# Attention, MLP and rotation dealt from one list of lines; normalisation with z on ScalarE, and fp32 transposes split into high and low halves as they leave PSUM

## What is computed

```python
# each of the three layers; shift, scale and gate: six rows per sequence from silu(cond) @ w_ada
h = layernorm(x) * (1 + scale1) + shift1
x = x + gate1 * (attention(h, 16 heads of 18) @ w_proj)
h = layernorm(x) * (1 + scale2) + shift2
# layer 0: 4 experts of 288 -> 1152 -> 288, weighted by the top 2 of 4 gates; layers 1 and 2: one MLP
x = x + gate2 * (gelu(h @ w1 + b1) @ w2 + b2)
# last: E = expm(skew matrix of silu(c) @ W.T + b), U from the QR decomposition of P, computed on the chip
out = x + (x @ U) @ ((E - 1) @ U.T)
```

## Time and profile before

| what | before |
|---|---|
| median of three runs | 1694.19 us (1693.63 to 1696.64) |
| the profiled execution's own time | 1697.5 us |
| its span, first to last instruction | 1695.8 us |
| mean granted TensorE clock | 0.917 |
| TensorE matmul busy | 1415.2 us, 83% of the span |
| DVE busy | 1051.0 us, 62% |
| ScalarE busy | 804.6 us, 47% |
| GpSimd busy | 346.3 us, 20% |
| HBM traffic | 61 GB/s over the span |

### The profile page before, as it was taken

How to read it: one execution, slowest core, us unless ns; L and a number is a source line. 1 busy time by engine, 2 the same in 40 slices (tenths; PEclk the granted TensorE clock), 3 DMA queues, 4 the chain that set the end, 5 groups by cost and what they waited for, 6 DMA issues and landing times. The chain is left out here.

```text
span 1695.8 us, 31116 instructions
## 1 busy us (share of the span) xinstructions
PE 1415.2 (83%) x12102; PEld 822.2 (48%) x12102; DVE 1051.0 (62%) x2500; ACT 804.6 (47%) x1519; POOL 346.3 (20%) x425
## 2 busy tenths in 40 slices
PE   3647897787899997999999999899886657897877
PEld 0324453443555553556566555565643424454445
DVE  4566654667687777766665464655656775667443
ACT  1443454365455656564625555545454442453542
POOL 0001031223323333223111222211220020121210
PEclk9768998888899998999999999999998878898988
DMA  4332233422111212123103123202020010100001
GB/s 129 87 129 69 63 97 104 152 97 70 59 41 72 80 55 71 48 87 108 17 27 99 52 87 108 57 33 68 8 67 18 19 60 6 33 7 19 19 21 43
DMA packets 79465, 105.35 MB, mean 62 GB/s; under 512 B 39237, under 2 KB 66390, under 8 KB 75990
## 3 DMA queue, kind: packets, MB, share of 16 engines
q1 hardware_dynamic: 77206, 100.99, 19.3%
q10 hardware_dynamic: 2112, 2.36, 0.4%
HBM read 86.57 MB, written 16.49 MB: 61 GB/s over the span
## 5 line engine op out<-in xcount | busy, mean ns | idle before, releaser
L1204 PE MATMUL P<-XT,W 128*128 128x512 f16 x1512 | 355.9, 387 | 0.4 <-ACT HQS L1949 0.4
L1350 PE MATMUL P<-W,H 128*128 128x288 f16 x864 | 255.9, 296 | 2.0 <-POOL H L2011 1.9
L1351 PE MATMUL P<-W,H 128*128 128x288 f16 x864 | 255.0, 295 | 0.0
L1352 PE MATMUL P<-W,H 128*128 128x288 f16 x864 | 254.8, 295 | 0.0
L2006 POOL TENSOR_TENSOR X<-X,TM 128x288 f32<-128x288 f32 x144 | 126.9, 884 | 602.2 <-DVE TM L1683 513.5
L1204 PEld LDWEIGHTS P<-XT,W 128*128 128x128 f16 x1512 | 142.9, 99 | 178.9 <-issue 27.6
L1941 ACT ACTIVATE G<-P 128x512 f32<-128x512 f32 x216 | 129.0, 597 | 120.5 <-PE P L1204 104.4
L1931 ACT ACTIVATE ARENA<-P 128x512 f32<-128x512 f32 x256 | 135.5, 602 | 86.9 <-PE P L1310 86.7
L1608 DVE TENSOR_REDUCE NM<-P 128x2 f16<-128x512 f32 x256 | 157.8, 685 | 15.1 <-PE P L1295 14.7
L2011 POOL TENSOR_TENSOR H<-G,H 128x512 f16<-128x512 f32 x100 | 120.2, 1205 | 194.4 <-ACT H L1942 189.5
L1204 PE MATMUL P<-WQ,XT 128*128 128x288 f16 x1008 | 145.7, 289 | 1.2 <-ACT XT L1863 0.5
(11 more groups left out here) (283 smaller groups left out, 2240.2 us busy)
## 6 DMA issues: line engine op xcount, KB each, us to landing
W<-scr_w SPq DMA_DIRECT2D x9, 1440.0 KB, 6.1
W<-scr_w SPq DMA_DIRECT2D x9, 1368.0 KB, 5.7
ADB<-scr_ada SPq DMA_DIRECT2D x24, 432.0 KB, 4.1
ADB<-scr_ada SPq DMA_DIRECT2D x24, 288.0 KB, 4.3
scr_w<-W SPq DMA_DIRECT2D x4, 1440.0 KB, 5.9
scr_w<-W SPq DMA_DIRECT2D x4, 1368.0 KB, 5.7
STG<-in_L_w SPq DMA_DIRECT2D x11, 432.0 KB
STG<-in_L_WT SPq DMA_DIRECT2D x11, 324.0 KB
```

The source lines that it names most:

```text
L1204: ins = e.matmul(o, l, r, start=k == 0, stop=k == len(pairs_) - 1)
L1350: e.matmul(o, hi, W2[:, 2 * m, :], start=False, stop=False)
L1351: e.matmul(o, hi, W2[:, 2 * m + 1, :], start=False, stop=False)
L1352: ins = e.matmul(o, lo, W2[:, 2 * m, :], start=False, stop=m == 8)
```

## The change

It has two parts.

The order. `attention`, `across` and `fence` go. One `deal` runs over seven lines and the MLP stream until nothing is left: all attentions in order of layer and batch (rank 0), what follows them (`settle` and `finish`, 0.5), the maxima (0.8), the preparations (1), the background (3) and two lines of the rotation (5). The stream's `up` has rank 2 and its `down` -1. A line may split into several (a tuple is yielded): q, k and v of both tiles run as six, the maxima as two. `slot` and `two` now also yield until the time at which the bank is reckoned free. `hold` and `release` let the exponentials of an attention (half of one in layers 0 and 2) and the GELUs of an `up` take turns. Buffers that one line holds for another are marked None until they are free. The arena shrinks by XB, and Z, MB and OUT of the rotation move to the two staging buffers STG, so that the rotation of a batch may begin when its chunk has left the last MLP.

The columns. `layernorm` makes z = x * r - mean * r on ScalarE, one pass per tile with scale and bias per token; GpSimd computes the bias in two more small instructions; the scale is one DVE pass over both tiles (576 elements), the shift one more on DVE or GpSimd, whichever the planner reckons sooner. `to_columns` transposes y in fp32, six transposes into two banks, and the split into high and low is made in reading PSUM: ScalarE writes the high half to XT, DVE subtracts it and writes the low half and the copy of the 32 last features. The rows of ones in XT are set once (`xt_ones`).

```diff
 def slot(ring):
-    while ring.held():
-        yield "wait"
+    return slots(ring, 1)
...
+def slots(ring, n):
+    asked = -1.0
+    while True:
+        free = sorted((f for f in ring.free if f is not None), key=ends)
+        if len(free) < n:
+            yield "wait"
+        elif ends(free[n - 1]) <= asked or not free[n - 1]:
+            return
+        else:
+            asked = ends(free[n - 1])
+            yield list(free[n - 1])
...
+        Z = [STG[i][0:D, 0:256] for i in range(2)]
+        MB = [STG[i][0:D, 256:256 + C] for i in range(2)]
+        OUT = [STG[i][:, 544:544 + 2 * C].rearrange("p (a c) -> p a c", c=C) for i in range(2)]
...
+        def hold(kind):
+            other = "gelu" if kind == "exp" else "exp"
+            turns["asks"].add(kind)
+            while turns["now"] or (turns["last"] == kind and (other in turns["asks"] or other == "gelu" and ms.half == 0 and ms.line())):
+                yield "wait"
+            turns["asks"].discard(kind)
+            turns["now"] = turns["last"] = kind
...
+        def to_columns(b, y, full, mixed=False):
+            yield from two(rP)
+            _, j, pf = rP.take()
+            _, j2, pf2 = rP.take()
+            m = do(pe, "xb_T", 0.7, y=y, js=(j, j2), full=full, free=[pf, pf2])
+            yield [m]
+            before = TR[2 * b] + TR[2 * b + 1]
+            hi = do(act, "x_hi", 1.0, b=b, mixed=mixed, js=(j, j2), src=m, free=before)
+            yield [hi]
+            lo = do(dve, "x_lo", 1.3, b=b, mixed=mixed, js=(j, j2), src=m, hi=hi, free=before)
...
-            p = do(pool, "ln_eps", 0.4, w=w, src=aggr, free=tok.get(("mv", w)))
+            p = do(pool, "ln_eps", 0.6, w=w, src=aggr, free=tok.get(("mv", w)))
             p = do(pool, "ln_pow", 0.8, w=w, src=p)
+            p = do(pool, "ln_mean", 0.4, raises="ln_pow", w=w, src=p)
+            z = do(act, "ln_z", 1.2, w=w, b=b, power=p, x=[XW[2 * b], XW[2 * b + 1]], free=free)
+            s = do(dve, "ln_scale", 0.76, w=w, sc=sc, src=z, rows=rows)
+            lane, cost = sooner([s], (pool, 1.5), (dve, 0.76))
+            r = do(lane, "ln_shift", cost, raises=f"ln_shift_{lane.name}", w=w, sh=sh, src=s)
...
-        def deal(need, others=(), stream=False):
-            while not all(x.over for x in need):
+        def deal(lines):
+            while True:
+                todo = [y for x in (*lines, *ms.line()) for y in x.tips()]
...
+        every = [(L, b) for L in range(3) for b in range(B)]
+        preps = Line(chain(*(chain(*[wq_load(L)] * (L > 0), *(prep(L, b) for b in range(B))) for L in range(3))), 1)
+        tops = Line(chain(*(maxima_tokens(b) if L == 1 else maxima_rows(L, b) for L, b in every)), 0.8)
+        attends = Line(chain(*(attend_tokens(b) if L == 1 else attend(L, b) for L in range(3) for b in range(B))), 0)
+        deal([attends, ends_, tops, preps, bg, *(Line(rotated(k), 5) for k in range(2))])
...
             def xb_T(st):
+                for n in range(2):
+                    for k in range(2):
+                        c = 256 * k + 128 * n
+                        e.transpose(P[j][:, c:c + 128], y[:, n, 128 * k:128 * k + 128], IDF[:, :])
+                    ins = e.transpose(P[j2][0:32, 128 * n:128 * n + 128], y[:, n, 256:C], IDF[:, :])
...
+            def x_lo(st):
+                for k, part_ in main:
+                    e.tensor_tensor(like(st, XT[:, 3:5, :][:, k, sl]), part_, like(st, XT[:, 0:2, :][:, k, sl]), ALU.subtract)
+                e.tensor_tensor(like(st, low), tail, like(st, high), ALU.subtract)
+                e.tensor_copy(same, high).then_inc(st.sem)
...
+            def ln_z(st):
+                e.activation(YL[w][:, 0, :], X[:, 2 * b, :], ACT.Identity, scale=RSS[w][:, 1, 0:1], bias=RSS[w][:, 0, 0:1])
+                e.activation(YL[w][:, 1, :], X[:, 2 * b + 1, :], ACT.Identity, scale=RSS[w][:, 1, 1:2], bias=RSS[w][:, 0, 1:2]).then_inc(st.sem)
```

More of the change, by code:

```diff
@@ L96, in chain @@
         yield from p
+def slots(ring, n):
[9 more added lines that the diff above has]
+            yield list(free[n - 1])
 def slot(ring):
-    while ring.held():
-        yield "wait"
+    return slots(ring, 1)
 def two(ring):
-    while sum(f is not None for f in ring.free) < 2:
-        yield "wait"
+    return slots(ring, 2)
 def part(g, n):
@@ L247, in program @@
         V1 = over([2, C])
-        XB = [over([2, 640], F16) for _ in range(2)]
         YL = [over([2, C]) for _ in range(2)]
@@ new lines, in prep_tokens, with maxima_tokens, maxima @@
+            while qt_rd[u] is None:
+                yield "wait"
+            yield tuple(turned(g, *x) for g in range(2) for x in (("q", full_q, qb_rd, qt_rd[u]), ("k", full_k, kb_rd, kt_rd[u])))
+            tok["turned", 1, b] = made
+            qt_rd[u] = kt_rd[u] = v32_rd[u] = None
+            yield
+        def maxima_tokens(b):
+            while ("turned", 1, b) not in tok:
+                yield "wait"
+            u, made, mx = b % 2, tok["turned", 1, b], []
+            def maxima(first):
+                for c in range(first, 4, 2):
+                    yield from two(rP)
@@ new lines, in heads @@
+                while qt_rd[u] is None:
+                    yield "wait"
+                yield from slot(rP)
+                _, j, pf = rP.take()
+                m = do(pe, "qk_T", mm_cost(8, 128), name=name, n=n, j=j, src=[a, d], free=pf, ind=tok.get("ind"))
+                last[n] = [m]
+                yield [m]
+                v = copy("qt" if name == "q" else "kt", 1.03 + BIAS, 0.7, u=u, n=n, j=j, src=m, free=(qt_rd if name == "q" else kt_rd)[u])
+                rP.free[j] = [v]
+                made.append(v)
@@ L1083, in wait, with line @@
                     yield "wait"
-            def line(self, half=None):
-                if half is not None and half != self.half:
-                    return []
+            def line(self):
                 if self.now is not None and not self.now.over:
@@ L1090, in line @@
                 if self.able():
-                    self.now = Line(self.piece(), 9)
+                    self.now = Line(self.piece(), 2 if self.half == 0 else -1)
                     return [self.now]
@@ L1113, in step @@
                     return
+                if isinstance(v, tuple):
+                    self.kids = [Line(g, self.rank) for g in v]
+                    for x in self.kids:
+                        x.when = self.when
+                    return
                 self.when = self.before if v == "free" else ends(v) if isinstance(v, list) else newest[0]
                 self.before = newest[0]
-        def deal(need, others=(), stream=False):
-            while not all(x.over for x in need):
-                lines = [x for x in (*need, *others, *(ms.line() if (stream() if callable(stream) else stream) else ())) if not x.over]
-                now = [x for x in lines if x.when <= pe.clock + SLACK]
-                best = min(now, key=lambda x: x.rank) if now else min(lines, key=lambda x: x.when)
-                best.step()
@@ L1124, in attention @@
-        def attention(L, before, first, after):
-            deal([first, *before], [bg], stream=L > 0)
-            for b in range(B):
-                fin = Line(finish(L, b - 1) if b else iter(()), 2 if L == 2 else 0, tok["o", b - 1] if b else ())
-                nxt = Line(prep(L, b + 1), 1) if b + 1 < B else after
-                at = attend(L, b)
-                for n in (16, 99):
-                    if L == 0:
-                        deal(ms.line(1), [fin, nxt, bg])
-                    deal(ms.line(0), [fin, nxt, bg])
-                    deal([Line(part(at, n), 0)], [fin, nxt, bg, *ms.line(1)])
-                deal([fin, nxt] if b + 1 < B else [fin], [bg], stream=lambda: b < B - 1 and nxt.waits)
@@ L1137, in across @@
-        def across(before, first, after):
-            deal([first], [bg, *before], stream=True)
-            for i in range(4):
-                rE1.free[i] = list(rE.free[i // 2])
-            for b in range(B):
-                fin = [Line(finish(1, b - 1), 0.5, tok["o", b - 1])] if b else before
-                nxt = [Line(prep(1, b + 1), 1)] if b + 1 < B else []
-                deal([*fin, *nxt, Line(attend_tokens(b), 0)], [bg] if b + 1 < B else [bg, after], stream=True)
-            for i in range(2):
-                rE.free[i] = [rE1.free[2 * i], rE1.free[2 * i + 1]]
@@ L1148, in fence @@
-        def fence():
-            return [lane.steps[-1] for lane in (pe, dve, act, pool)]
+        def deal(lines):
+            while True:
+                todo = [y for x in (*lines, *ms.line()) for y in x.tips()]
+                if not todo:
+                    return
+                now = [x for x in todo if x.when <= pe.clock + SLACK]
+                best = min(now, key=lambda x: x.rank) if now else min(todo, key=lambda x: x.when)
+                best.step()
         def retire():
```

441 lines of the change are left out of this document (230 added, 211 removed).

## The result

The changed kernel takes **1638.78 us**, the median of four runs (1637.58 to 1640.54), against 1694.55 us for the kernel before beside it (1693.63 to 1696.64): a ratio of 0.967, 95% interval 0.9653 to 0.9687. It is faster by 56 us, 3.3%. The forecast was 1550, a gain of 144: the time lies inside the range of 1470 to 1670, but only 56 of the 144 us came. The profiled execution took 1638.8 us with a span of 1636.8.

A forecast was written before the change was run, and what follows sets the result against it. TensorE was taken to bound the middle stage, the order of work the rest. 120 + 270.2 + 800.3 + 308.5 + 8.5 + 45 = 1552.5 us of span, put at 1550 for the median; range 1470 to 1670.

The forecast's parts named there:

- What bounds it: TensorE bounds the middle stage; before and after it the order does, in the last layer through waits behind the maxima.
- B: Rival: chains stay in line, the last layer keeps its 405 us, only front and tail gain; 1680 us, chance 0.15.
- C: Rival: slower, lines queue for the eight PSUM banks and the longer chains come into the open; 1730 us, chance 0.13.
- A: The sum itself: weak stages move towards the middle stage's rate; 1510 to 1600 us, chance 0.60.
- The work: TensorE's busy time times clock over the whole kernel stays within 2% of 1313.5 us plus 8.
- The two weak stages: 120 to 440 and 1240 to 1645 us: joint rate from 0.687 to 0.861, 146.3 us less; bounds 0.80 and 0.919.
- The first GELU: Sign at the front: the first GELU, at 207.7 us in the kernel before, comes before 170 us.
- stretches of 48 us: Sign late in the kernel: no stretch of 48 us after 1200 us has a clock under 0.9.
- The middle stage stays at its own rate: 800.3: 440 to 1240 us, MLP beside token attention: rate 0.919 kept, so 800.3 us in the sum.
- The tail: After the last attention: 50.8 us becomes 45, bounds 35 and 51, as first batches' rotations go beside the last attention.
- The columns: Normalisation and transposes: 8.5 us more TensorE time; other engines only bounded; chains 2 us longer, 96 us if uncovered, taken as covered.
- The lock of the two engines: SBUF passes on VectorE and GpSimd exclude each other: 24 shifts on POOL could delay DVE by at most 42 us.

The follow-up runs named there:

- order_only: The changed kernel's new order with the old normalisation and old columns (two XB buffers back): 1658.29 us.
- columns_only: The kernel before, its order kept, with the new `layernorm` and `to_columns`: 1705.91 us.
- mlp_next_only: The changed kernel with one planner rule changed: where no line is ready, the MLP's line counts as ready 2 us sooner than the others: 1652.30 us.
- bg_rank09: The changed kernel with the background line at rank 0.9 instead of 3, ahead of the preparations and `up`: 1679.62 us.
- hh_cost3: The changed kernel with the planner reckoning a Householder step's VectorE arithmetic at 3.0 us instead of 2.3, same work: 1631.89 us.
- mlp_next_29: The changed kernel, settling line first, MLP reckoned 1.8 us sooner, Householder arithmetic 2.9 us, margin 1.3 us, background and rotations at ranks 1.8 and 2.1: 1608.64 us.

## Why the prediction was partly right

**What bounds it: right.** The last layer did stand behind its maxima, and does no longer (50.1 us to 3.6 at the lines that waited for them). In the changed kernel's timeline a Householder step and fourteen `up` matmuls stand between two groups of score matmuls (line 1383):

```profile
1316.01 0.76 PE L1383 MATMUL P<-KT,QT 64*128 64x256 f16 x8 [0.38 <-ACT HQS L2035]
1318.67 1.07 PE L1415 MATMUL P<-IDF,OT 128*128 128x128 f32 x8 [1.91 <-DVE XT L1594]
1321.81 0.99 PE L1455 MATMUL P<-AT,IDF 64*64 64x228 f32 x2 [2.07 <-DVE NM L1693]
1322.73 5.21 PE L1288 MATMUL P<-XT,W 128*128 128x512 f16 x14
1327.87 0.39 PE L1383 MATMUL P<-KT,QT 64*128 64x256 f16 x4
```

The mechanisms of rivals B (the order does little) and C (the banks stand in the way) do not occur: of TensorE's waits in the middle stage none is for the copies out of the transposes, and in the last layer the copies (lines 1594 and 1943) keep it waiting for 8.9 us. The time itself, 1638.78, lies between the range of A, which ends at 1600, and B's 1680.

**The work: right.** 1330.8 us against the 1321.3 of the sum, within 1%. The fp32 transposes are 0.11 us apart, as forecast: in the changed kernel's timeline, where each row is a run of matmuls,

```profile
1328.47 0.27 PE L1306 MATMUL P<-IDF,ARENA 128*32 128x128 f32 x1
1328.58 0.38 PE L1305 MATMUL P<-IDF,ARENA 128*128 128x128 f32 x2
1328.80 0.27 PE L1306 MATMUL P<-IDF,ARENA 128*32 128x128 f32 x1
```

**The two weak stages: within their bounds, 34 us slower than the value taken.** The forecast had them at 0.861, bounds 0.80 and 0.919. They reach 252.3 + 286.3 = 538.6 us of work in 660 us, 0.816: at 0.861 they would take 27 us less up to 440 and 7.5 less after 1240. Two signs failed here. The first GELU comes at 184.7 us, where I had said before 170; it came at 207.7. And of the stretches of 48 us from 1200 us on, 1296 to 1344 has a clock of 0.89 and 1536 to 1584 one of 0.86, where I had said none under 0.9.

**"The middle stage stays at its own rate: 800.3": the step that failed.** It was put down without bounds below 0.919, as if a rate were a property of the mixture of work. It is one of the order. The MLP does fill TensorE beside attention in the old order; in the new one much the same mixture (31 of the last layer's 128 maxima stand in the stage, where there were 10) reaches 0.866: 46 us of the 84 by which the span exceeds the sum. `order_only` has the loss (0.854) and `columns_only` has not (0.922), so it comes with the order. Of the two waits that grew, one is at Householder steps: the fallback puts them in front of matmuls that could go, as the timeline at 972 us shows. The other is for the DMA of the row of maxima. `mlp_next_only` changes the fallback alone, both waits shrink, and the stage is back at 0.911. How much of that is the step's own hole and how much the order that moved with it, no run separates; leaving 56 of the steps out gives 0.899. The time of `mlp_next_only` also shows why the middle stage can't be taken by itself, since the chain that is pushed back there comes out at the end.

**The tail: 12 us longer.** 45 us were forecast; the stage after 1580 has 56.8. The rotations of the first batches do not go beside the last attention, since E isn't ready. It is the last thing that the background line computes, after the Householder steps, which end at 1381 us. The last squaring of E (line 1806) and the first product of the rotation (line 1504; each row gives the first and the last start):

```profile
L1806 DVE SCALAR_TENSOR_TENSOR EY<-EX,P x6: 686/689/690, 1532.2 to 1560.0; 128x512 f32<-128x512 f32 x6
L1504 PE MATMUL P<-UT,EY x16: 402/453/740, 1560.8 to 1623.0; 64*64 64x288 f32 x16
```

In the kernel before E was there at 893 us. The forecast freed the rotation's arrays and left the rank of what feeds it out of account. The background line that falls behind is common to this and to the middle stage; that it comes in time is not enough, as `bg_rank09` shows.

The excesses, 27 + 46 + 7.5 + 12, make 92 us; the span is 84.3 above the 1552.5 of the sum. The first stage gives some back, as it holds 56.6 us of work in its 120 us, not 43.6.

**The columns: right in their bounds, of no certain worth.** VectorE ends at 1002.6 us (forecast 1025), ScalarE at 794.0 (below 875), GpSimd at 393.2 (below 475). "Covered" was nearly right: 10 us net come out in the old order, of 96. In the new order they gain 19.5 us, which I hadn't forecast and can't assign to a mechanism. A change of one cost in the plan (`hh_cost3`) moves the time by 7 us and one rank (`bg_rank09`) by 41, so a difference of 20 between two greedy orders may be the order's and not the columns'.

**The lock of the two engines: rare, and not where I had put it.** The copy at line 1594 reads and writes SBUF:

```profile
L1594 DVE COPY XT<-XT x72: 217/218/1354, 43.9 to 1628.9; 32x256 f16<-32x256 f16 x72
```

218 ns at the median and 1354 at most, 1.14 us more. Beside that one GpSimd runs a subtraction of 1.14 us (line 2108). By the rule of the Trainium skill (SBUF — State Buffer, "SBUF: two separate sides") whoever starts first holds the other off for its whole instruction; the trace agrees here. (The page says so of VectorE instructions with two inputs in SBUF or in a mode with two ports; the copy has one input, and no row shows its mode.) It need not be one only: in the kernel before, an instruction of 152 ns took 2.21 us beside two subtractions on GpSimd, one behind the other,

```profile
656.66 2.26 POOL L2011 TENSOR_TENSOR H<-G,H 128x512 f16<-128x512 f32 x2
656.72 2.21 DVE L1731 SCALAR_TENSOR_TENSOR HS<-HS,N 64x1 f32<-64x1 f32 x1 [0.73 <-POOL N L2021]
```

so one instruction of VectorE can lose two of GpSimd. The 1454 ns of the earlier trace rows, too, stand beside such a subtraction (1154 ns), and not beside an addition to x. Over the whole kernel it went the other way than the 42 us that I had allowed. Adding up what VectorE's instructions take beyond the median of their line and shape, where that is over a quarter, gives 26 us, against 44 in the kernel before. All 40 of these instructions, and all 57 before, overlap one of GpSimd. 25 of the 44 us stand in the small instructions of the Householder steps and 18 in the old normalisation and columns; of the 26, 8 and 6. In `mlp_next_29` it is 68 us, 50 of them in the Householder steps: the order decides what meets, and a step's length with it.

**Open.** Why rank and margin gain 61 us together and nothing apart; why the wait for the DMA of the row of maxima shrinks with the fallback; how far below 1572 us this work can be ordered; what part of the change's own 56 us is its order's luck.

## What to carry over

- A rate read from one stage of a profile belongs to the order that made it. If a change replaces the order, put bounds on the strong stages as on the weak ones.
- In a list that each engine runs in order, a dependent chain that fills a gap on a guess costs its own wait on top (up to 4.3 us for a step here). Ask what the planner takes when nothing is ready, and whether that item's time is real or only an upper mark.
- What stands at the end of a low-ranked line may be what the last stage needs. Look up when each input of the tail is ready before the tail is forecast.
- A greedy order answers to tiny changes with tens of us (here 1572 to 1680 from a few planner numbers). Judge such a change by what it does to a named wait, and time several neighbours before a part is given the credit.

## What the runs showed of the hardware

ScalarE's z pass was taken at 0.409 us, from a copy of the same 288 columns out of PSUM. With scale and bias per partition, from SBUF, it takes half as much again:

```profile
L1948 ACT ACTIVATE ARENA<-X,RS 128x288 f32<-128x288 f32 x48 | 30.1, 628 | 36.9 <-POOL RS L2093 36.8
L1949 ACT ACTIVATE ARENA<-X,RS 128x288 f32<-128x288 f32 x48 | 29.8, 621 | 0.0
```

The source and the operands both differ here, so no run shows which of them costs the 0.21 us. The Trainium skill (ScalarE: Activation LUTs, "What ACT_TABLE_LOAD costs") gives an ACTIVATE 186 ns and 0.833 ns for each column, and some 93 ns more for each operand that points to a column of values: 612 ns with two of them, as an estimate from that page. The trace's 621 and 628 agree. For a z pass that is 21 us more of ScalarE than I had allowed, and it cost nothing: ScalarE has half its time free.

A pass over 32 partitions costs VectorE no less than one over 128 for 256 columns out of PSUM, 414 ns and 417. So the last 32 features take 48.9 us (lines 1593 and 1594) of the 98.6 us of the low half, near the 110 allowed:

```profile
L1593 DVE TENSOR_TENSOR XT<-P,XT 32x256 f16<-32x256 f32 x72 | 29.8, 414 | 1.0
...
L1592 DVE TENSOR_TENSOR XT<-P,XT 128x256 f16<-128x256 f32 x16 | 6.0, 417 | 4.2 <-ACT XT L1943 3.6 <-issue 0.6
```
